# Attention kernel: values and exponent sums from one set of matmuls, ones interleaved among V's columns

## The reference, cut to what matters

```
x = x + xattn(layernorm(x), ctx_1024, ctx_1024, mask, Wq, Wk, Wv, Wo)
x = x + attn(layernorm(x), Wq, Wk, Wv, Wo, W_down_kv, W_up_k, W_up_v)
x = x + ffn(layernorm(x), w1, b1, w2, b2)

# xattn                                              # attn
scores = einsum('bhqd,bhkd->bhqk', Q, K)/sqrt(8)     scores = clip(qk/(sqrt(128)+1e-8)) * decay
attn = softmax(where(masked, -inf, scores))          attn = softmax(clip(scores))
out = einsum('bhqk,bhkd->bhqd', attn, V) @ Wo        out = einsum('bhqk,bhkd->bhqd', attn, vh) @ Wo
```

## Time and profile before

| | |
|---|---|
| span of the profiled execution | 311.6 us |
| three runs | 313.46, 311.86, 311.66 us |
| PE busy | 286.9 us, 92% |
| DVE busy | 255.7 us, 82% |
| ACT busy | 240.9 us, 77% |
| POOL busy | 227.7 us, 73% |
| TensorE's clock, mean granted | 0.981 of full |

### The profile page before, as it was taken

The page is one execution under the profiler, slowest core; times in us unless marked ns, Lnnn a source line. Parts: engine busy times, 40 slices in busy tenths (PEclk is TensorE's granted clock), DMA queues, the critical chain, the costliest instruction groups (busy, mean ns, idle before and its releaser), DMA issues.

```text
span 311.6 us, 13655 instructions
## 1 busy us (share of the span) xinstructions
PE 286.9 (92%) x5744; PEld 197.9 (64%) x5744; DVE 255.7 (82%) x558; ACT 240.9 (77%) x530; POOL 227.7 (73%) x185
## 2 busy tenths in 40 slices
PE   7788879999999999999999999999999999699592
PEld 2355547676767777675868676767677768343182
DVE  2897679999888888887888887877888998789773
ACT  3585858585869888787888888898978877799590
POOL 5676569797998877799999999999899972230000
PEclk9999999999999999999999999999999999989778
DMA  7999000000000000000000000000000000000027
GB/s 232 307 285 286 12 2 4 2 2 5 4 2 2 4 2 3 5 2 2 4 2 5 3 4 2 5 3 2 5 2 4 2 5 4 1 0 2 0 72 200
DMA packets 16542, 11.64 MB, mean 37 GB/s; under 512 B 5153, under 2 KB 14690, under 8 KB 16482
## 3 DMA queue, kind: packets, MB, share of 16 engines
q1 hardware_dynamic: 15762, 10.34, 12.1%
q10 hardware_dynamic: 720, 0.43, 0.5%
HBM read 8.67 MB, written 2.10 MB: 35 GB/s over the span
## 4 chain that ended last, share of the span: by engine, by line
PE 71%; DVE 15%; issue 5%; ACT 4%; DMA 3%; POOL 1%; SPq 1%; DVEq 0%; POOLq 0%
PE ps L588 12%; PE ps L569 10%; PE ps L615 10%; PE ps L621 8%; PE ps L631 8%; DVE hmax L1119 5%; PE ps L586 4%; PE ps L505 4%; PE ps L497 4%; PE ps L484 3%; PE ps L600 3%; DVE u L1038 3%; DMA arena<-in_mask_BxS_if 2%; DMA out<-pt 1%; DVE stats L949 1%
## 5 line engine op out<-in xcount | busy, mean ns | idle before, releaser
L840 ACT ACTIVATE pt<-ps 128x512 f32<-128x512 f32 x128 | 75.9, 593 | 21.6 <-PE ps L588 20.8
L414 POOL TENSOR_TENSOR u<-u,mx 128x1024 f32<-128x1024 f32 x32 | 60.9, 1903 | 24.9 <-DVE mx L1057 24.6
L406 POOL TENSOR_TENSOR ud<-u,con 128x1024 f32<-128x1024 f32 x31 | 73.5, 2371 | 1.4 <-DVE u L1043 1.4
L1038 DVE SCALAR_TENSOR_TENSOR u<-ps,rs,arena 128x1024 f32<-128x1024 f32 x32 | 40.9, 1279 | 13.6 <-PE ps L569 12.1
L1043 DVE TENSOR_SCALAR u<-ps 128x1024 f32<-128x1024 f32 x32 | 39.0, 1220 | 12.3 <-PE ps L569 11.9
L569 PE MATMUL ps<-arena,qT 32*64 32x256 f32 x1024 | 44.0, 399 | 5.0 <-DVE u L1038 2.5
L615 PE MATMUL ps<-pt,vx 128*32 128x64 f32 x2048 | 41.3, 221 | 2.9 <-DVE oT L979 1.3
L615 PEld LDWEIGHTS ps<-pt,vx 128*32 128x32 f32 x2048 | 32.4, 110 | 16.5 <-issue 11.1
L621 PE MATMUL ps<-pt,con 128*32 128x128 f32 x1024 | 40.0, 273 | 1.2 <-issue 1.2
L1057 DVE TENSOR_REDUCE mx<-u 128x16 f32<-128x1024 f32 x32 | 38.7, 1210 | 0.1
L569 PEld LDWEIGHTS ps<-arena,qT 32*64 32x64 f32 x1024 | 14.9, 129 | 31.3 <-issue 21.6
(11 more groups left out here) (154 smaller groups left out, 549.6 us busy)
## 6 DMA issues: line engine op xcount, KB each, us to landing
out<-pt SPq DMA_DIRECT2D x8, 256.0 KB, 3.1
arena<-in_ctx_cols SPq DMA_DIRECT2D x4, 256.0 KB, 4.6
xn3T<-in_x_cols SPq DMA_DIRECT2D x4, 256.0 KB, 4.8
x<-in_x SPq DMA_DIRECT2D x4, 256.0 KB, 5.4
arena<-in_ctx_cols SPq DMA_DIRECT2D x2, 512.0 KB, 6.7
xn3T<-in_x_cols SPq DMA_DIRECT2D x2, 512.0 KB, 6.2
x<-in_x SPq DMA_DIRECT2D x2, 512.0 KB, 7.7
arena<-in_mask_BxS_if SPq DMA_DIRECT2D x2, 256.0 KB, 6.4
```

Of the source, the lines that this page charges most:

```text
L406: pool.tensor_tensor(dh, uh, decay.unsqueeze(1).to_broadcast([P, H, HALF]), ALU.mult)\
L414: pool.tensor_tensor(uh, uh, mx[:, n % 4, 0:count].unsqueeze(2).to_broadcast([P, count, HALF]), ALU.subtract)\
L840: act.activation(pt[:, n % 2, 4 * half:4 * half + 4].rearrange("p h n -> p (h n)"), ps[:, bank, :], ACT.Exp).then_inc(s["emptied"], 1)
L1038: dve.scalar_tensor_tensor(by_head(u[:, n % UB]), sc, rs[:, 0, n:n + 1], mask[:, n].unsqueeze(1).to_broadcast([P, H, HALF]), ALU.mult, ALU ...
```

## The change: what it does, and the diff

For tiles 0 to 61 (`WHOLE` = 62) the weights of each L615 matmul hold V in every second column and ones in the others: 64 columns for a head pair, 32 for each parity, V on even columns for parity 0 and on odd ones for parity 1. The 8 matmuls with `ones` (L621) are gone for these tiles. Each parity writes its own 128 columns of PSUM, no longer accumulating; two tiles alternate in the bank. The output has numerators and sums on alternating partitions: even partitions hold numerators in parity 0 and sums in parity 1, odd ones the other way round.

ACT copies both blocks (128 partitions x 256 columns) from PSUM to `raw` (`take_out`). SP then issues four transfers (`align`), each 64 partitions x 128 columns (32 KB) from SBUF to SBUF: two bring the sums to the partitions of their numerators, two bring the numerators of both parities together, in `nd`. `raw` and `nd` have three slots. Ln reads the sums from `nd`, one turn later than before (LAG_DEN), and the division reads both operands from SBUF; projection and residual follow one turn later. Tiles 62 and 63 keep the old way, with weights in `vl`. The heads' columns come out in another order, so the rows of Wo are permuted before the launch.

On ACT a turn now begins with Ln of the tile before and then the copy of this one. On SP the transfers of tiles 0 to 3 stand among the loads. POOL's memset of `vx` is cut in three: POOL clears slot 0, DVE slots 1 and 2, POOL writes the ones (12 memsets). POOL's sum of weights (L393) moves from turn 4 to turn 7; a memset of `vl` comes in turn 20.

```diff
@@ -39,15 +39,15 @@
-ROOT_TURN = ((-1, 1, 4, 7, 12, 17), tuple(15 + 4 * g for g in range(8)), (46, 54, 62, 65, 67, 69))
+ROOT_TURN = ((-1, 1, 4, 7, 12, 17), tuple(15 + 4 * g for g in range(8)), (47, 55, 63, 66, 67, 69))
-APPLY3 = (50, 52, 58, 60, 63, 65, 67, 70)
+APPLY3 = (50, 52, 58, 60, 64, 66, 67, 70)
-EARLY = NS - 4
+LAST_ADD = NS + 5
...
@@ -60,7 +60,11 @@
-LAG_T, LAG_SHIFT, LAG_PV, LAG_ADD = 2, 3, (3, 4), (4, 5)
+LAG_T, LAG_SHIFT, LAG_PV, LAG_DEN = 2, 3, (3, 4), (4, 5)
+WHOLE = NS - 2
+LAG_MOMENTS = 10
+RAW = 3
+VW = 64
...
@@ -82,7 +86,7 @@
-            (col[None, :] // DH) == (2 * par + p // HALF)[:, None]
+            (col[None, :] % 2 == par) & (col[None, :] // (2 * DH) == (p // HALF)[:, None])
...
@@ -94,6 +98,27 @@
+def den_turn(n):
+    return n + (LAG_PV[1] if n >= WHOLE else LAG_DEN[n // NT])
+def divided(turn):
+    return [n for n in range(NS) if den_turn(n) == turn]
+def added(turn):
+    return [n for n in range(NS) if den_turn(n) + 1 == turn]
+def moments3(turn):
+    return [n - NT for n in added(turn) if n >= NT]
+def variances3(turn):
+    return [t for t in range(NT) if turn == den_turn(NT + t) + (2 if t < NT - 3 else 1)]
...
@@ -133,7 +158,10 @@
-        vx = sb("vx", [P, RING3, 2, GT, RG, 3, 16])
+        vx = sb("vx", [P, RING3, 2, GT, RG, VW])
+        vl = sb("vl", [P, 1, 2, NS - WHOLE, RG, VW])
+        raw = arena[:, 14336:15104].rearrange("p (s a n) -> p s a n", s=RAW, a=2)
+        nd = arena[:, 15104:15872].rearrange("p (s a n) -> p s a n", s=RAW, a=2)
...
@@ -257,6 +286,10 @@
+        def num(n, par):
+            return 2 * P * (n % 2) + P * par
         def num_den(n):
...
@@ -264,6 +297,16 @@
+        def aligned(n):
+            return 32 * (n // RAW + 1)
+        def columns_of(v, slot, e, first, between):
+            pitch, blocks = v.shape[1] * v.shape[2] * v.shape[3] * RG * VW, v.shape[3] * RG
+            return [bass.AP(v[:, :, :, :, :, :].tensor, HALF * e * pitch + (2 * slot + b) * blocks * VW + 2 * DH * e + first,
+                            [[pitch, HALF], [VW, blocks], [between, 2], [2, DH]]) for b in range(2)]
...
@@ -290,19 +333,35 @@
+            def align(n):
+                slot = n % RAW
+                sp.wait_ge(s["raw_done"], n + 1)
+                if n >= RAW:
+                    sp.wait_ge(s["o_ready"], n - RAW + 1)
+                sp.dma_start(nd[0:P:2, slot, 1], raw[1:P:2, slot, 0]).then_inc(D_IN[slot], 16)
+                sp.dma_start(nd[1:P:2, slot, 1], raw[0:P:2, slot, 1]).then_inc(D_IN[slot], 16)
+                sp.dma_start(nd[0:P:2, slot, 0], raw[0:P:2, slot, 0]).then_inc(N_IN[slot], 16)
+                sp.dma_start(nd[1:P:2, slot, 0], raw[1:P:2, slot, 1]).then_inc(N_IN[slot], 16)
             load(2)
             load(3)
             load_mask(2)
             load(4)
+            align(0)
             for dst, src in ((wq[:, 1], sWq), (wkv_raw[:, 0], sWk), (wkv_raw[:, 1], sWv),
...
+            align(1)
             load_mask(3)
+            align(2)
             load(5)
+            align(3)
             for dst, src in ((w1r[:, :, :], w1_in.rearrange("(p c) d -> p c d", p=P)), (w2r[:, :], w2_in),
+            for n in range(4, WHOLE):
+                align(n)
             for m, g in enumerate(DOWN):
...
@@ -311,7 +370,15 @@
         def _(pool):
-            pool.memset(vx[:, :, :, :, :, :, :], 0.0).then_inc(s["vx_zeroed"], 1)
+            pool.memset(vx[:, 0], 0.0).then_inc(s["vx_zero"], 1)
+            pool.wait_ge(s["vx_zero"], 1)
+            for slot in range(RING3):
+                if slot == 1:
+                    pool.wait_ge(s["vx_cleared"], 1)
+                for e in range(2):
+                    for block in columns_of(vx, slot, e, 1, 31):
+                        pool.memset(block, 1.0).then_inc(s["vx_ones"], 1)
+            pool.wait_ge(s["vx_ones"], 4 * RING3)
...
@@ -388,7 +455,9 @@
-                if n == 4:
+                if n == 20:
+                    pool.memset(vl[:, :, :, :, :, :], 0.0).then_inc(s["vl_zeroed"], 1)
+                if n == 7:
...
@@ -608,12 +677,21 @@
                 if 1 <= n < NS - 1:
-                    pe.wait_ge(s["o_ready"], n)
+                    pe.wait_ge(s["raw_done"], n)
+                if n < WHOLE:
+                    for b in range(2):
+                        for par in range(2):
+                            for r in range(RG):
+                                last = pe.matmul(ps[32 * r:32 * (r + 1), bank, num(n, par) + HALF * b:num(n, par) + HALF * (b + 1)],
+                                                 vx[:, j % RING3, b, i, r, 32 * par:32 * (par + 1)],
+                                                 pt[:, n % 2, 2 * r + par, HALF * b:HALF * (b + 1)], start=True, stop=True)
+                    last.then_inc(s["pv_done"], 1)
+                    return
                 for b in range(2):
-                                      vx[:, j % RING3, b, i, r].rearrange("p c m -> p (c m)")[:, 16 * par:16 * par + 32],
+                                      vl[:, 0, b, n - WHOLE, r, 32 * par:32 * (par + 1)],
...
@@ -794,16 +872,22 @@
                 if kind == "v":
-                    if j == 0:
-                        act.wait_ge(s["vx_zeroed"], 1)
+                    if j < RING3:
+                        act.wait_ge(s["vx_ones"], 4 * (j + 1))
                     if j >= RING3:
-                    for b in range(2):
-                        for e in range(2):
+                    if j == 2 * NG - 1:
+                        act.wait_ge(s["vl_zeroed"], 1)
+                    whole = GT - (NS - WHOLE) if j == 2 * NG - 1 else GT
+                    for e in range(2):
+                        blocks = columns_of(vx, j % RING3, e, 0, 33)
+                        tail = columns_of(vl, 0, e, 0, 33)
+                        for b in range(2):
-                            dst = vx[HALF * e:HALF * (e + 1), j % RING3, b].rearrange("p t r c m -> p (t r) c m")
-                            last = act.copy(dst[:, :, 0:3:2, DH * e:DH * (e + 1)], src)
+                            last = act.copy(blocks[b][:, 0:whole * RG], src[:, 0:whole * RG])
+                            if whole < GT:
+                                last = act.copy(tail[b], src[:, whole * RG:])
                 if kind == "wr":
...
@@ -840,9 +924,22 @@
+            def take_out(n):
+                act.wait_ge(s["pv_done"], n + 1)
+                if n >= RAW:
+                    act.wait_ge(D_IN[n % RAW], aligned(n - RAW))
+                    act.wait_ge(N_IN[n % RAW], aligned(n - RAW))
+                act.copy(raw[:, n % RAW].rearrange("p a n -> p (a n)"), ps[:, OB, num(n, 0):num(n, 0) + 2 * P])\
+                    .then_inc(s["raw_done"], 1)
             def log_den(n):
-                act.wait_ge(s["pv_done"], n + 1)
-                act.activation(lden[:, n % 2], ps[:, num_den(n), P:2 * P], ACT.Ln).then_inc(s["ln_done"], 1)
+                if n < WHOLE:
+                    act.wait_ge(D_IN[n % RAW], aligned(n))
+                    act.activation(lden[:, n % 2], nd[:, n % RAW, 1], ACT.Ln).then_inc(s["ln_done"], 1)
+                else:
+                    act.wait_ge(s["den_ready"], n - 1)
+                    act.wait_ge(s["pv_done"], n + 1)
+                    act.activation(lden[:, n % 2], ps[:, num_den(n), P:2 * P], ACT.Ln).then_inc(s["ln_done"], 1)
...
@@ -876,11 +973,18 @@
+                for tile in divided(n):
+                    if tile < WHOLE:
+                        log_den(tile)
                 for tile in due(n, LAG_PV):
-                    log_den(tile)
+                    if tile < WHOLE:
+                        take_out(tile)
+                for tile in divided(n):
+                    if tile >= WHOLE:
+                        log_den(tile)
                 if 0 <= n - LAG_T < NT:
-                for tile in due(n, LAG_PV):
+                for tile in divided(n):
...
@@ -937,6 +1041,7 @@
+            dve.memset(vx[:, 1:RING3], 0.0).then_inc(s["vx_cleared"], 1)
...
@@ -976,8 +1081,10 @@
-                dve.tensor_tensor(oT[:, n % 2], ps[:, num_den(n), 0:P], rden[:, n % 2], ALU.mult)\
-                    .then_inc(s["o_ready"], 1)
+                if n < WHOLE:
+                    dve.wait_ge(N_IN[n % RAW], aligned(n))
+                dve.tensor_tensor(oT[:, n % 2], nd[:, n % RAW, 0] if n < WHOLE else ps[:, num_den(n), 0:P], rden[:, n % 2],
+                                  ALU.mult).then_inc(s["o_ready"], 1)
...
@@ -1056,26 +1163,26 @@
-                for tile in due(n, LAG_PV):
-                    if tile not in (EARLY, NS - 1):
+                for tile in divided(n):
+                    if tile < NS - 1:
-                    divide(EARLY)
-                for k, lag in ((1, 10), (2, LAG_ADD[1] + NT)):
-                    if 0 <= n - lag < NT:
-                        moments(k, n - lag)
-                    if 0 <= n - lag - 1 < NT - 2 * (k == 2):
-                        variance(k, n - lag - 1)
-                    if k == 2 and NT - 2 <= n - lag < NT:
```

(27 more changed lines are left out.)

## The result

The changed kernel takes 342.06 us (median of 4 runs, 340.51 to 342.93) against 312.0 us of the kernel before, measured beside it: a ratio of 1.094 with the interval 1.090 to 1.098. The forecast of 306.9 us and its range up to 315 were wrong. The profiled execution spans 338.6 us against 311.6.

The account below looks back on a forecast made before the run. PE was taken to bound the kernel, with POOL also full in part of layer 1. Terms -3.2 - 0.9 - 1.5 + 0.6 = -5.0 us gave a span of 306.6, 306.9 us on the median's scale; range 300 to 315.

Parts of the forecast that it names:

- The division at "same price": DVE's division, reading both operands from SBUF, keeps 0.281 us for each of 64; bounds 0.2 and 0.56 (a doubling).
- Rival B: Each division stops POOL for 0.28 us, lengthening POOL's layer-1 turns; about 315 us, chance 0.08.
- SP's queue: SP's loads, waiting behind the transfers at the start, cost nothing; Ln might wait once, up to 3 us.
- a gain of 1.5: Start to turn 8 (43.25 us): between -3.1 and +1.8 us, taken as -1.5.
- The loop through the transfers: Copy, transfer issue, landing of 2.0 us, Ln and wakes on ACT and SP: 3.34 us, shorter than the turn.
- Rival A: The loop through the transfers sets the turn, from a landing of 2.5 us; 323 to about 346 us, chance 0.2.
- The tail, +0.6: Last tiles: Ln(62) comes 1.2 us later behind Ln(61), PE's 1.2 us less gives half back; +0.6 us.
- L621 at 0.625 us a tile: Removing the denominators' matmuls takes 0.625 us a tile off PE, 38.8 us over tiles 0 to 61.
- The steady-state gain: Turns 8 to 23 lose 3.2 us, layer 1 from 195.44 us loses 0.9; the stages between 0.
- rival C: PE not worth removing: DVE, ACT, POOL equally late, the copy eats L621's gain; about 309.4 us, chance 0.2.
- The copy: ACT's new 128x256 copy out of PSUM takes 0.38 us a tile, 23.6 us over 62 tiles.
- V's copy: ACT's scatter of V into every second column keeps its 0.367 us for each of 64; upper end a doubling.

Follow-up runs that it names:

- without any transfer: The version with all three edits, without its transfers: Ln and the division read ACT's copy in place, unaligned; 308.43 us, ratio 0.987.
- all three edits: The changed kernel with the reciprocal in PSUM, the copy put ahead of Ln, and SP's loads spread at the start; 316.04 us, ratio 1.010.
- three tail tiles: The version with all three edits, with tile 61 too on the old way (no transfers for the last three tiles); 314.44 us, ratio 1.008.

## Why the prediction was wrong

- **The division at "same price", 0.281 us (the failed step).** It was given bounds of 0.2 and 0.56. It took 0.854 in the mean and 5.07 at most. Its bound by "a doubling" assumed that a contention slows two accesses by a factor; what happens is a wait until POOL is done, so the bound should have been POOL's instruction, 1.9 to 2.4 us (L414 in layer 0, L406 in layer 1). 19.0 of the 30 us go with this one operand, and 20.4 us come with it in the kernel before.
- **Rival B had the right place and the wrong victim.** It let POOL pay 0.28 us a turn (315 us). POOL's decay kept its 2.37 us ("L475 ... | 73.7, 2377" on the page; right behind a held division it took up to 2.44), and DVE paid. The Trainium skill (GPSIMD Engine Reference, Specifications) names this contention with two SBUF inputs; the trace agrees, and shows who waits here and how long. The prediction priced one direction alone; 62 waits of up to 2 us in the second one would have moved the forecast.
- **SP's queue, "I cost this at nothing", at most 3 us once.** It was 4.30 and 4.28 us, at tiles 1 and 3, and turn 8 came 5.0 us late where a gain of 1.5 was forecast. Spreading the loads brought turn 8 forward by 2.7 us, and without any transfer it came 2.9 us earlier than in the kernel before. The prediction asked only when the moved loads would arrive, not what they do to the small transfers behind them.
- **The loop through the transfers was sized rightly.** Landing 2.0 us: measured 1.7 to 1.9 in the median. Issue 0.48: measured 0.47 for the first and 0.60 for the others, so 2.3 us a tile instead of 1.9. The section of the Trainium skill that the prediction drew on for 2.0 us (DMA: Bandwidth & Descriptors, Anatomy of one DMA) describes transfers that POOL issues; for these, issued by SP, the trace's own number stands. Rival A, which had 0.2, gave a time near the measured one for the wrong reason: halving the wait ahead of Ln brought no more than 1.3 us. A rival's time that fits does not prove its mechanism.
- **The tail, +0.6.** Up to the last residual it was +5.4, and +5.7 in the version with all three edits; without the transfers still +3.0, with three tiles in the old way +4.0. So the transfers in turns of 2.5 us, the place that was named, account for 2.7 us, over twice the 1.2 us that I counted as the delay of one logarithm. The other 3.0 us have no term in the sum and stand without transfers too. That the division and the residual come a turn later is the obvious suspect; no run tests it.
- **L621 at 0.625 us a tile.** With all three edits PE is busy 270.2 us against 286.9: 16.7/62 = 0.27 us a tile. Starts in the trace before show why; PE's rows of one tile in order of time:
```profile
183.19 0.62 PE L615 MATMUL ps<-pt,vx 128*32 128x64 f32 x32
183.63 0.61 PE L621 MATMUL ps<-pt,con 128*32 128x128 f32 x16
184.17 0.49 PE L631 MATMUL ps<-wo,oT 128*128 128x128 f32 x2
```
  From L615 to the projection it is 0.98 us here; the repaired kernel has 181.80 to 182.38, 0.58, and both are typical (medians 1.02 and 0.58). The removal saves 0.40 us, as groups overlap and their busy times can't be added. It was worth two fifths to two thirds of what I took.
- **The steady-state gain** was forecast as 3.2 + 0.9 us. With all three edits it is 1.5 in layer 0 and 1.5 in layer 1, so it was there, smaller at first and larger later: rival C was close here. From turn 8 to 23, where DVE was to set the turn and 3.2 us were to go, it was 0.4. Why layer 0 gains no more, with PE, DVE, ACT and POOL busy 82.6, 79.3, 77.2 and 77.2 of 88.7 us, is not settled.
- **Small terms.** The copy: 0.364 us for 0.38. V's copy: 0.389 for 0.367. The memsets hid: the first score reader starts at 10.5 us, before at 10.2. The clock was forecast unchanged; its granted mean fell from 0.981 of full to 0.955. From 48.26 to 106.51 us it is 0.93, a mix of the two levels 1.2 and 2.4 GHz, in a stretch in which PE is busy 49.1 of 58.25 us with gaps ahead of its groups; from 43.60 to 132.30 in the version with all three edits it is 1.00. The lowest part follows ACT's second long wait: PE was busy 3.02 of the 8.26 us up to 48.26, and then 10.1 of 10.7 us at a granted 0.78. In the start the lower clock cost 1.5 us with all three edits and 2.4 with three tail tiles; over the whole run it was not priced.

## What to carry to other kernels

Before a DVE instruction gets a second SBUF operand, look at what POOL runs beside it, and price a wait for the whole of that instruction; where a PSUM operand is to be had, keep it. A small transfer that an engine waits for needs a place in the queue that is free of large loads before it, and one hides in a steady turn but not in a start or tail with shorter ones. Read what a removed group is worth from the distance of the starts around it, not from its busy time.
